# Splitting the gate products, gating the projection weights chunk by chunk, holding GpSimd during the norm's small products, projecting the lower half first, and a new timetable

## The reference: two layers of a small image network

```
# layer 0
h = silu(bn1(w_exp @ ln_c(x)))                   # 96 -> 576 channels
h = silu(bn2(depthwise3x3(h)))
s = sigmoid(w_se2 @ silu(w_se1 @ mean(h) + b_se1) + b_se2)   # 576 -> 24 -> 576: the gate
x = x + ln_c(x) + bn3(w_proj @ (h * s))          # 576 -> 96
x = x + ffn(ln_t(x))                             # 96 -> 384 -> 96, rounded to fp8e5 and fp16
# layer 1
g = gelu(gn(w1 @ ln_c(x) + b1))                  # gn: one mean and variance over the whole image
y = gelu(w21 @ a(g)+b21) + gelu(w21 @ b(g)+b21) + gelu(w22 @ c(g)+b22) + gelu(w22 @ d(g)+b22)
x = x + w3 @ gn(y) + b3                          # a, b, c, d: g shifted by one row or column
x = x + ffn(ln_t(x))
```

## Time and profile before

| | |
|---|---|
| three timed runs | 5884.94, 5888.1, 5890.72 us; median 5888.1 us |
| profiled execution | 5895.56 us, of which the span from first to last instruction 5893.7 us |
| TensorE busy | 5303.1 us (90%) |
| VectorE busy | 4892.0 us (83%) |
| ScalarE busy | 4145.5 us (70%) |
| GpSimd busy | 574.4 us (10%) |
| mean granted TensorE clock | 0.945 of full |

### The profile page before, as it was taken

The page is one execution under the profiler, slowest core; times in us unless marked ns, Lnnn a source line. Parts: engine busy times, 40 slices in busy tenths (PEclk is TensorE's granted clock), DMA queues, the critical chain, the costliest instruction groups (busy, mean ns, idle before and its releaser), DMA issues.

```text
span 5893.7 us, 165528 instructions
## 1 busy us (share of the span) xinstructions
PE 5303.1 (90%) x67266; PEld 2773.9 (47%) x67266; DVE 4892.0 (83%) x8119; ACT 4145.5 (70%) x7517; POOL 574.4 (10%) x431
## 2 busy tenths in 40 slices
PE   1889999999999999999999999999999998999986
PEld 0344555444555444555444555444555444555442
DVE  4878988888988888988888988888988888988874
ACT  1467766677867677777767867767867777867766
POOL 1111001111001111001111001111001111001100
PEclk9999999999999999999999999999999999999997
DMA  1334434444433444443444434445443445443433
GB/s 51 84 100 122 105 99 103 116 116 125 105 100 101 115 115 122 105 102 102 117 115 126 102 101 104 118 111 126 102 102 102 116 114 125 104 101 100 113 79 78
DMA packets 467883, 625.04 MB, mean 106 GB/s; under 512 B 81218, under 2 KB 466691, under 8 KB 467035
## 3 DMA queue, kind: packets, MB, share of 16 engines
q1 hardware_dynamic: 467132, 614.44, 41.2%
HBM read 272.13 MB, written 78.68 MB: 60 GB/s over the span
## 4 chain that ended last, share of the span: by engine, by line
PE 51%; issue 24%; DVE 8%; ACT 6%; POOL 6%; DMA 3%; SPq 1%; POOLq 0%; ACTq 0%; DVEq 0%
PE bank L596 21%; PE bank L650 11%; PE b_banks L596 7%; POOL x_in L1110 6%; PE bank L637 4%; PE sums_b L603 3%; PE sums_a L603 2%; DVE conv L965 2%; DMA x_in<-in_x 2%; ACT hidden L879 2%; PE bank L679 1%; ACT hidden L886 1%; DVE bn_stats L1037 1%; PE bank L666 1%; PE bank L660 1%
## 5 line engine op out<-in xcount | busy, mean ns | idle before, releaser
L965 DVE SCALAR_TENSOR_TENSOR conv<-mid,w_dw,conv 128x1568 f32<-128x1568 f32 x1280 | 2339.8, 1843 | 3.6
L761 PE MATMUL b_banks<-shifted,w_combo 128*32 128x392 f32 x6144 | 639.8, 543 | 179.8 <-DMA shifted<-g 115.7
L596 PE MATMUL bank<-xc_a,w_exp 128*32 128x392 f32 x5376 | 714.8, 509 | 43.7 <-DVE xc_a L948 38.7
L1110 POOL TENSOR_TENSOR x_in<-x_in,xc_a 96x392 f32<-96x392 f32 x256 | 509.7, 2000 | 1731.4 <-DVE xc_a L948 1125.4
L679 PE MATMUL bank<-conv,w_proj_gated 128*32 128x392 f32 x1920 | 665.7, 503 | 0.0
L596 PE MATMUL bank<-conv,w_proj_gated 128*32 128x392 f32 x5760 | 652.7, 495 | 0.2 <-DVE w_proj_gated L979 0.2
L596 PE MATMUL bank<-x,centering 128*32 128x392 f32 x4608 | 646.3, 504 | 1.5 <-ACT sq_a L790 0.5
L650 PE MATMUL bank<-phases,w_toeplitz 128*32 128x392 f32 x6144 | 645.1, 494 | 0.8 <-ACT phases L823 0.7
L879 ACT ACTIVATE hidden<-b_banks 128x1176 f16<-128x1176 f32 x512 | 590.6, 1153 | 40.5 <-PE b_banks L596 36.9
L637 PE MATMUL bank<-xc_a,w_exp 128*32 128x448 f32 x4096 | 593.6, 545 | 15.8 <-ACT mid L816 15.4
L886 ACT ACTIVATE hidden<-hidden 128x1176 fp8e5<-128x1176 f16 x512 | 607.3, 1186 | 0.8 <-PE bank L596 0.7
(11 more groups left out here) (165 smaller groups left out, 9279.0 us busy)
## 6 DMA issues: line engine op xcount, KB each, us to landing
phases_on<-phases SPq DMA_DIRECT2D x1024, 101.5 KB, 2.4
shifted<-g SPq DMA_DIRECT2D x512, 149.6 KB, 2.7
x_in<-in_x SPq DMA_DIRECT2D x512, 147.0 KB, 2.7
shifted<-g SPq DMA_DIRECT2D x256, 199.5 KB, 3.0
...
```

The lines of the kernel that those rows point to most:

```text
L596: last = mm(o[j:j + QUAD, :], weights[:, j:j + QUAD], x, start=start, stop=stop)
L761: last = mm(rows(PB[32 * u:32 * u + 32, m, 0:TW]), WC[:, u // 2, 32 * m:32 * m + 32], SH[t % 2][:, u, :].rearrange("p (h w) -> p h w", w=G ...
L965: v.scalar_tensor_tensor(out=acc, in0=src, scalar=WDW[:, k, j:j + 1], in1=acc, op0=ALU.mult, op1=ALU.add).then_inc(convolved, 1)
L1110: g.tensor_tensor(xl, xl, xc_tile(t), ALU.add).then_inc(sem["xplus_a"], 1)
```

## The change

1. **Gate products.** The 21 products are in two steps: se1a makes the 20 whose sums are there before the last SiLU of VectorE's chunks, se1 the last one. They accumulate in a column of their own in the bank sums_a (SE1P) and take no ring bank. The second gate product is issued as 20 column strips of 32 channels with 32 contraction rows, and its bias is a 25th row of the weights against a constant 1, so that VectorE's addition goes. ScalarE's tanh reads PSUM directly.
2. **Weights chunk by chunk.** Half of the projection weight is kept in WP; VectorE makes `WPS = WP * tanh + WP` in six operations of 96 columns (L985), each with a count of its own, and a projection product waits for its chunk alone. That takes the place of L972, L977 and L979.
3. **GpSimd held.** After the power, GpSimd waits for the norm's scale and offset before it goes on.
4. **Lower half first.** `turned(t) = (t + 4) % 8`: the projection, x1, the centring and variance of ln_t that follow, the reload and the last store start with tile 4. The first tap of the next image's chunk 0 on the lower half (L962) waits for three projection tiles in place of six.
5. **New timetable.** All numbers of TIMES are new.

```diff
--- before.py
+++ after.py
...
-        "rstd_a": (5168,), "norm_a": (5622, 5814, 5991, 6773, 6831, 7212, 7671, 7960),
+        "rstd_a": (5343,), "norm_a": (6239, 6376, 7121, 7321, 7393, 7558, 7910, 8129),
...
     VPS = {"a": small_a[C:C + VR, 0:VW], "c": small_a[C:C + VR, 128:128 + VW], "b": small_b[C:C + VR, 0:VW]}
+    SE1P = small_a[0:SEH, 200:201]
     GNP = small_b[0:C, 400:404]
...
         return NPR * image + (NTH - 1) * h + min(r, NTH - 2) + 1
+    def turned(t):
+        return (t + NTH) % NT
...
                 t = arg[0]
-                u = NTH * (t // NTH) + (0, NTH - 1, 1, 2)[t % NTH]
+                u = turned(NTH * (t // NTH) + (0, NTH - 1, 1, 2)[t % NTH])
                 sp.wait_ge(s_stored[u % XSLOTS], at(16 * (NT // XSLOTS * a + u // XSLOTS + 1)))
...
             elif name == "store":
-                t = arg[0]
-                sp.wait_ge(sem["ffn_added"], at(ffn(1, e) + t + 1))
+                t = turned(arg[0])
+                sp.wait_ge(sem["ffn_added"], at(ffn(1, e) + arg[0] + 1))
                 sp.dma_start(out[e, :, t * TW:(t + 1) * TW], tile(XA, t)).then_inc(stored[t], 16)
...
                 last.then_inc(sem["t_convolved"], 1)
-            elif name == "se1":
-                pe.wait_ge(sem["activated2"], at(N_S2 * (a + 1)))
-                pe.wait_ge(sem["t_activated2"], at(N_TC * (a + 1)))
-                wait_bank(pe, prev)
+            elif name in ("se1a", "se1"):
                 chunk_of = [0] + [k for k in range(1, NDV) for _ in range(2)] + [0] * PH + [NDV] * (2 * PH) + [NCH] * PH
-                for j, k in enumerate(chunk_of):
-                    last = mm(ring[bank][C:C + SEH, 0:1], SE1[:, k, :], SUMS[:, j:j + 1], start=(j == 0), stop=(j == len(chunk_of) - 1))
-                last.then_inc(sem["se_matmul"], 1)
+                late = N_S2 - 1
+                if name == "se1a":
+                    pe.wait_ge(sem["activated2"], at(N_S2 * a + late))
+                    pe.wait_ge(sem["t_activated2"], at(N_TC * (a + 1)))
+                    pe.wait_ge(sem["se_scalar"], at(2 * a - 1))
+                    for j, k in enumerate(chunk_of):
+                        if j != late:
+                            mm(SE1P, SE1[:, k, :], SUMS[:, j:j + 1], start=(j == 0), stop=False)
+                else:
+                    pe.wait_ge(sem["activated2"], at(N_S2 * (a + 1)))
+                    mm(SE1P, SE1[:, chunk_of[late], :], SUMS[:, late:late + 1], start=False, stop=True)\
+                        .then_inc(sem["se_matmul"], 1)
             elif name == "se2":
...
                 for k in range(NCK):
-                    last = mm(ring[bank][:, k:k + 1], SE2[:, 128 * k:128 * k + 128], S1, start=True, stop=True)
+                    last = columns(ring[bank][:, k:k + 1], SE2[:, 128 * k:128 * k + 128], S1)
                 last.then_inc(sem["se_matmul"], 1)
...
                 h, r = divmod(arg[0], NTH - 1)
-                if arg[0] == 0:
-                    pe.wait_ge(sem["se_vector"], at(3 * (a + 1)))
                 wait_bank(pe, prev)
                 for k in range(NCH + 1):
-                    weights = WPS[:, k if k < NCH else NCH + h, :]
-                    maps = conv(k, h) if k < NCH else ACC4
+                    if r == 0 and (h == 0 or k == NCH):
+                        pe.wait_ge(sem["se_vector"], at((NCK + 1) * a + (k + 1 if h == 0 else NCK + 1)))
+                    weights = WPS[:, k if k < NCH else NCH + 1 - h, :]
+                    maps = conv(k, 1 - h) if k < NCH else ACC4
                     start, stop = k == 0, k == NCH
...
                 act.wait_ge(sem["se_matmul"], at(2 * a + 1))
-                f(S1, ring[bank][C:C + SEH, 0:1], ACT.Silu, scale=1.0 / NPOS, bias=BSE1).then_inc(sem["se_scalar"], 1)
-            elif name == "se3":
-                act.wait_ge(sem["se_vector"], at(3 * a + 1))
-                f(GATE[:, 1, :], GATE[:, 0, :], ACT.Tanh, scale=0.5).then_inc(sem["se_scalar"], 1)
+                f(S1[0:SEH, :], SE1P, ACT.Silu, scale=1.0 / NPOS, bias=BSE1[:, :]).then_inc(sem["se_scalar"], 1)
+            elif name == "se2":
+                act.wait_ge(sem["se_matmul"], at(2 * a + 2))
+                act.wait_ge(sem["se_vector"], at((NCK + 1) * a))
+                f(GATE[:, :], ring[bank][:, 0:NCK], ACT.Tanh, scale=0.5).then_inc(sem["se_scalar"], 1)
             elif name == "center":
...
                         act.wait_ge(sem["varsummed_a"], at(NT * (n + 1)))
-                    act.wait_ge(sem["normed_f"], at(ffn(0, a - 1) + t + 1 if a else 0))
+                    act.wait_ge(sem["normed_f"], at(ffn(0, a - 1) + turned(t) + 1 if a else 0))
                     act.wait_ge(sem["varsummed_c"], at(NT * a + t - 1))
                     act.wait_ge(sem["centered_c"], at(NT * a + t + 1))
-                    center_out(o, tile(XC0, t), SQA[t % 2][0:C, :], "squared_c")
+                    center_out(o, tile(XC0, turned(t)), SQA[t % 2][0:C, :], "squared_c")
                 else:
...
                     if k <= 1:
-                        dve.wait_ge(sem["projected"], at(NPR * m))
+                        dve.wait_ge(sem["projected"], at(NPR * (m - 1) + NTH - 1 if h else NPR * m))
                     v.tensor_scalar(acc, src, WDW[:, k, j:j + 1], None, ALU.mult).then_inc(convolved, 1)
...
                                            op0=ALU.mult, op1=ALU.add).then_inc(convolved, 1)
-            elif name == "se2":
-                dve.wait_ge(sem["se_matmul"], at(2 * a + 2))
-                v.tensor_tensor(GATE[:, 0, :], ring[bank][:, 0:NCK], BSE2[:, :], ALU.add).then_inc(sem["se_vector"], 1)
             elif name == "se3":
                 dve.wait_ge(sem["se_scalar"], at(2 * a + 2))
-                v.tensor_scalar(GATE[:, 2, :], GATE[:, 1, :], 0.5, 0.5, ALU.mult, ALU.add)\
-                    .then_inc(sem["se_vector"], 1)
-                dve.wait_ge(sem["se_vector"], at(3 * a + 2))
                 dve.wait_ge(sem["projected"], at(NPR * a))
-                v.tensor_tensor(WPS[:, 0:NCK, :], WP[:, 0:NCK, :],
-                                GATE[:, 2, :].unsqueeze(2).to_broadcast([128, NCK, C]), ALU.mult)
-                v.tensor_scalar(WPS[CW:128, NCK, :], WP[CW:128, NCK, :], GATE[CW:128, 2, NCH:NCK], None, ALU.mult)\
-                    .then_inc(sem["se_vector"], 1)
+                for k in (*range(NCH), NCK, NCH):
+                    p0, p1, g = (CW, 128, NCH) if k == NCK else (0, CW, k) if k == NCH else (0, 128, k)
+                    v.scalar_tensor_tensor(out=WPS[p0:p1, k, :], in0=WP[p0:p1, k, :], scalar=GATE[p0:p1, g:g + 1],
+                                           in1=WP[p0:p1, k, :], op0=ALU.mult, op1=ALU.add).then_inc(sem["se_vector"], 1)
             elif name == "x1":
...
                 k = arg[0]
-                t, u = NTH * h + r, NTH * h + NTH - 1
+                t, u = turned(NTH * h + r), turned(NTH * h + NTH - 1)
                 dve.wait_ge(stored[t], at(16 * (a - 1)))
...
                 g.tensor_tensor(col(GY), col(GV), HALVED[:, :], ALU.pow).then_inc(sem["gn_rstd"], 1)
+                pool.wait_ge(sem["gn_affine"], at(GN_P * (2 * b + arg[0] + 1)))
             elif name == "norm_a":
...
         then(v.tensor_tensor(y3r, y3r, bn3_rows[:, 0:C], ALU.mult))
+        then(v.tensor_scalar(y3r, y3r, 0.5, None, ALU.mult))
         then(v.tensor_tensor(WP[:, 0:NCK, :], WP[:, 0:NCK, :], y3r.unsqueeze(1).to_broadcast([128, NCK, C]), ALU.mult))
...
```

91 lines of the change are left out of this document (46 added, 45 removed), and 104 rows, old and new, of the table TIMES.

## The result

| | before | changed |
|---|---|---|
| median of the timed runs, us | 5889.4 (4 runs, 5884.9 to 5903.1) | **5652.0** (4 runs, 5648.4 to 5660.6) |
| ratio, 95% interval | 1 | **0.9595** (0.9575 to 0.9615) |
| span of the profiled execution, us | 5893.7 | 5647.4 |
| mean granted clock | 0.945 | 0.974 |

A forecast was written before the change was run, and what follows sets the result against it. TensorE, 90% busy with 11% of the span at the lower clock, was taken as the bound, gains expected around the second norm and gate. 29 + 32 + 16 = 77 us off 5895.6 gave 5818.6, on the median 5811 us; range 5725 to 5885.

The forecast's parts named there:

- I expect the falls to stay: After the second norm: TensorE's clock still falls, as the new order packs se1a, se1 and both averages into 3 to 4 us.
- the clock comes back: Rival, after the second norm: less waiting prevents the clock's fall in half the images, 72 us more, 5740 us; chance 0.16.
- My own sign of being wrong: Mean clock, forecast at 0.945 +- 0.005: the prediction is wrong if it changes by more than 0.01.
- GpSimd held, -29 us: Second norm: undisturbed small VectorE operations cut TensorE's waits from 2.96 to 2.0 us, -0.9 us per image.
- Second gate product, -32 us: Gate: 40 records of 32 channels hold TensorE 1.0 us less per image; bounds -14 and -64 us.
- The first gate product: Gate: its 1.45 to 1.63 us do not shorten but move into the second norm's wait, already counted.
- Lower half first and the order, -16 us: Next image's taps and FFN stretch: a quarter of ScalarE's 70 us centring wait reaches TensorE, -0.5 us per image.
- the second fall: Stretch after the second norm, 3042 to 3052: clock 0.83, 3.4 us at 1.2 GHz in the profiled image.
- the gate chain: VectorE's gating: about 1.5 us shorter, but worth nothing, as TensorE has no idle time there.
- the collision: GpSimd's tile sums slowing VectorE: can return at the last weights' scaling, ready 1.8 us after the offset, hidden with little to spare.
- the dense stretch: 2900 to 2984, half of the period: TensorE busy 83.58 of 84 us at full clock, to stay unchanged.
- se1 doesn't block: Rival said se1's wait for the last SiLU blocks TensorE, slower, 5923 us with that SiLU at 9 us; chance 0.09.

The follow-up runs named there:

- e1: The changed kernel's code with the order table of the kernel before, the added step se1a placed right ahead of se1: 5707.1 us.
- e5: The kernel before with only GpSimd's wait for the norm's offset added: 5730.2 us.
- e3: The changed kernel without GpSimd's wait for the norm's offset: 5736.2 us.
- e7: The kernel before plus four dense products that nobody reads, ahead of TensorE's wait for the second norm's offset: 5772.4 us.
- e10: The changed kernel with the first gate product in one piece again, all 21 products waiting for the last SiLU: 5721.1 us.
- e2: The code of the kernel before with the changed kernel's order table, upper half still projected first: 6225.9 us.
- e9: The kernel before with GpSimd's wait added, plus dense products that nobody reads in TensorE's waits ahead of the FFN's low-clock period: 5696.6 us.

## Why the prediction was wrong

- **What failed: "I expect the falls to stay".** The rival *the clock comes back* was what happened, and I gave it 0.16. I had written beside it that a row of one-column products counts as little load, and that 1.70 us of waiting stood before each fall, and still took the falls as given because the new order packs se1a, se1 and both averages together. The low time at the gate fell from 290 to 129 us in the changed kernel and to nothing but the run's end in e1 and e5. My own sign of being wrong, a clock that moves by more than 0.01, came: 0.945 to 0.974. The packing may cost something, but far too little to keep the falls: from 10 us ahead of the bias product to 4 us behind it TensorE idles 1.5 us per image in e1 and in the changed kernel alike, and the low time at the gate is 38 us with the old order and 129 with the new one. No run shows that the packing is the cause.
- **GpSimd held, -29 us.** Mechanism right, size wrong: alone it is some 165 us (e5), in the changed kernel 84 (e3). I priced the wait as the wait only. It also lengthened the low time behind it, 134 us of busy time in e5. The wait itself was mis-sized as well: I had the stretch wait 2.0 us in place of 2.96, with ScalarE's SiLU late. Ahead of se1 it is 0.45 us, the bias product's 55.0 us became 1.5, and in the same 14 us TensorE idles 1.5 us per image in place of 3.1, which makes 49 us in place of my 29.
- **Second gate product, -32 us.** The strips take 17.6 / 32 = 0.55 us, where I took 1.0. The estimate by the Trainium skill (TensorEngine Tiling (Array Packing), Performance Considerations) was 1.0 as well, and the measurement differs from it. The product alone gave 47 us, of which some 23 were the low clock itself, which I had taken as the product's own price: in e7, where the clock around the gate stays up, the wide form takes 41.7 / 32 = 1.3 us. With the clock behind it, the strips are worth 97 us on the kernel before and 62 in the changed one.
- **The first gate product** I put at nothing beyond the wait. The split is worth 69 us (e10). In one piece the product waits 49.2 us, where the split one waits 13.8; in all TensorE's idle time grows by 55 us and its busy time by 15.
- **Lower half first and the order, -16 us.** 55 us (e1 against the changed kernel), inside my bounds of +30 to -70, all of it idle time, as the prediction had it. The wait that I named, ScalarE's last centring for its variance product, went from 70.0 us (58.1 in e1) to 0.2; I counted a quarter of it. That the order moves low time from the FFN to the gate and gains nothing by the clock was not foreseen, nor that it needs the lower half first (e2).
- **Only the second fall was looked at.** The windows of the earlier trace rows showed clock 0.89 in the FFN stretch. Its low time fell too, from 287 to 92 us; in e9 the time got some 40% of the arithmetic half of such low time.
- **Right:** the gate chain and the gating are hidden (only weight loads wait for the gated weights, 6.6 us in the whole run), the collision comes back at the scaling of the last weights and is hidden, the dense stretch is unchanged, the small operations are at 0.15 us, and se1 doesn't block.

The edit parts that were not taken alone are the gating chunk by chunk and the lower half without the order. e1 differs from e5 by 23 us, and the strips at full clock are worth 1.3 - 0.55 us, 24 us over 32 images; so in the old order the others, the split among them, are worth about nothing together. That is worked out, not measured.
